# First norm of a decoder layer in two halves of the tokens, with the first weights loaded ahead of the context

## The reference

```python
x = x + attn(layernorm(x), ...)        # 16 heads of 128: q, k through a causal depthwise convolution of 4 taps,
                                       # silu and a norm; a decaying state S = (1-b) S + b v k^T; gate; Wo
x = x + xattn(layernorm(x), ctx, ...)  # query and key from ctx (128 wide), softmax over 256, applied to x
x = x + ffn(layernorm(x), ...)         # 2 shared and 16 routed experts, 4 of 16 chosen per token
```

## Time and profile before

| what | us |
|---|---|
| median of three runs | 595.95 |
| the profiled execution's own time | 597.41 |
| its span | 595.5 |
| TensorE busy | 557.4 (94%) |
| VectorE busy | 437.1 (73%) |
| ScalarE busy | 398.3 (67%) |
| GpSimd busy | 298.9 (50%) |

### The profile page before, as it was taken

The page is one execution under the profiler, slowest core; times in us unless marked ns, Lnnn a source line. Parts: engine busy times, 40 slices in busy tenths (PEclk is TensorE's granted clock), DMA queues, the critical chain, the costliest instruction groups (busy, mean ns, idle before and its releaser), DMA issues.

```text
span 595.5 us, 10331 instructions
## 1 busy us (share of the span) xinstructions
PE 557.4 (94%) x3392; PEld 488.2 (82%) x3392; DVE 437.1 (73%) x1046; ACT 398.3 (67%) x783; POOL 298.9 (50%) x201
## 2 busy tenths in 40 slices
PE   3899999999999999999999999897777799999996
PEld 1687889989989989989989988786566688888885
DVE  8778989989989988998998998968593433333334
ACT  4978988878978979879779778665531433343331
POOL 2434756746746646656666563301041655556542
PEclk9998999999999999999999999999998899999999
DMA  6122032032032032032031020110002433333311
GB/s 206 29 107 81 0 117 81 1 116 81 2 117 81 2 116 81 2 116 75 8 116 56 27 97 23 59 29 1 0 1 70 149 105 107 104 123 113 108 62 70
DMA packets 16267, 42.23 MB, mean 71 GB/s; under 512 B 4544, under 2 KB 4800, under 8 KB 16224
## 3 DMA queue, kind: packets, MB, share of 16 engines
q1 hardware_dynamic: 16224, 41.69, 20.9%
HBM read 40.47 MB, written 1.21 MB: 70 GB/s over the span
## 4 chain that ended last, share of the span: by engine, by line
PE 83%; DVE 8%; ACT 4%; DMA 2%; issue 2%; SPq 1%; ACTq 0%; DVEq 0%
PE bank L1258 20%; PE bank L1260 19%; PE bank L1259 19%; PE bank L1254 15%; PE bank L1396 5%; PE bank L1384 4%; ACT tok L624 2%; DMA xbias<-in_xb 1%; DMA w_raw<-in_w 1%; DVE stats L976 1%; DVE xT_lo L911 1%; DVE gated_lo L1158 1%; ACT values L538 0%; DVE x L1248 0%; DVE raw L995 0%
## 5 line engine op out<-in xcount | busy, mean ns | idle before, releaser
L1258 PE MATMUL bank<-xT_lo,w_hi 128*128 128x512 f32 x336 | 140.0, 417 | 3.6 <-DVE conv L1149 1.3
L1260 PE MATMUL bank<-xT_hi,w_hi 128*128 128x512 f32 x336 | 132.3, 394 | 0.0
L1259 PE MATMUL bank<-xT_hi,w_lo 128*128 128x512 f32 x336 | 131.8, 392 | 0.0
L425 POOL TENSOR_TENSOR gated_lo<-gated,gated_hi 128x512 fp32r<-128x512 f32 x30 | 38.7, 1290 | 116.5 <-ACT gated_hi L644 112.8
L624 ACT ACTIVATE tok<-bank,nmr,rstd 128x128 f32<-128x128 f32 x256 | 91.0, 504 | 2.1 <-DVE nmr L891 2.1
L502 POOL TENSOR_TENSOR gate<-conv,tap 128x512 f32<-128x512 f32 x36 | 46.4, 1291 | 84.5 <-DVE conv L1149 71.4
L1258 PEld LDWEIGHTS bank<-xT_lo,w_hi 128*128 128x128 f32 x336 | 63.5, 189 | 18.8 <-DVE conv L995 3.2
L1260 PEld LDWEIGHTS bank<-xT_hi,w_hi 128*128 128x128 f32 x336 | 63.3, 188 | 14.2
L420 POOL TENSOR_TENSOR conv<-tap,conv 128x506 f32<-128x506 f32 x32 | 61.9, 1934 | 21.8 <-DVE conv L995 21.8
L420 POOL TENSOR_TENSOR raw<-tap,raw 128x506 f32<-128x506 f32 x32 | 61.9, 1934 | 20.3 <-DVE raw L995 16.3
L1259 PEld LDWEIGHTS bank<-xT_hi,w_lo 128*128 128x128 f32 x336 | 63.7, 190 | 9.6
(11 more groups left out here) (167 smaller groups left out, 1358.3 us busy)
## 6 DMA issues: line engine op xcount, KB each, us to landing
w_raw<-in_w SPq DMA_DIRECT2D x34, 384.0 KB, 4.4
obet<-obet_rows SPq DMA_DIRECT2D x16, 768.0 KB, 4.2
tap<-route_rows SPq DMA_DIRECT2D x16, 512.0 KB, 3.6
wv_raw<-in_wv SPq DMA_DIRECT2D x8, 256.0 KB, 4.8
wo_raw<-in_wo SPq DMA_DIRECT2D x8, 256.0 KB, 4.9
x<-in_x SPq DMA_DIRECT2D x2, 512.0 KB, 4.6
out_x<-x SPq DMA_DIRECT2D x4, 256.0 KB, 2.4
raw<-in_ctx SPq DMA_DIRECT2D x1, 512.0 KB, 5.4
```

The costliest lines, as they stand in the source:

```text
L425: nc.gpsimd.tensor_tensor(gated_lo[:, cc], gated[:, c * N:(c + 1) * N], gated_hi[:, cc].bitcast(F32), ALU.subtract).then_inc(gated_lo_read ...
L1258: nc.tensor.matmul(o, l_hi, r_lo, start=start, stop=False, skip_group_check=loose)
L1259: nc.tensor.matmul(o, l_lo, r_hi, start=False, stop=False, skip_group_check=loose)
L1260: return nc.tensor.matmul(o, l_hi, r_hi, start=False, stop=stop, skip_group_check=loose)
```

## The change

Nothing is computed in another way; instructions and loads change places.

- SyncE: the identity, head 0's weights and the first value weights are issued right behind x; the context's three loads follow, then the parameters, beta's weights and bias.
- VectorE: statistics and factors are made for half 0 alone (four tiles), then its norm and its low part, then the same for half 1. The mask's copies move from behind the norm to behind head 0's second taps, the low part of half 1 and of beta's weights between its first and second taps.
- ScalarE: the norm of half 0 and its copies come right behind the weights' high part; the norm of half 1, then the first taps of head 0, then half 1's copies.
- TensorE: the transposes of half 0, two context products, the query product of half 0, values unit 0, the transposes of half 1, values unit 1, the other two context products, and the query product of half 1.
- The context products use banks 4 and 5 twice, since banks 6 and 7 now hold values; products 2 and 3 wait until ScalarE has emptied the bank.
- GpSimd waits for the factors of half 0 only before its first low parts, and for both before the low part of head 1's weights.

```diff
--- before.py
+++ after.py
@@ -270,12 +270,7 @@
         def _(sp):
             for c in range(NCH):
                 sp.dma_start(x[:, c * T:(c + 1) * T], x_in[:, c * T:(c + 1) * T]).then_inc(ld_x[c], 16)
-            sp.dma_start(xw, xw_in).then_inc(ld["ctx"], 16)
-            sp.dma_start(ctxT, ctx_in).then_inc(ld["ctx"], 16)
-            sp.dma_start(xb[:, :], xb_in).then_inc(ld["ctx"], 16)
             sp.dma_start(ident[:, :], ident_in).then_inc(ld["const"], 16)
-            sp.dma_start(wb, wb_in).then_inc(ld["beta"], 16)
-            sp.dma_start(bb, bb_in).then_inc(ld["beta"], 16)
 
             def load_weights(g, k):
                 s = k % 2
@@ -315,8 +310,13 @@
                              ).then_inc(ld["wo"], 16)
 
             load_weights(0, 0)
+            load_values(0, 0)
+            sp.dma_start(xw, xw_in).then_inc(ld["ctx"], 16)
+            sp.dma_start(ctxT, ctx_in).then_inc(ld["ctx"], 16)
+            sp.dma_start(xb[:, :], xb_in).then_inc(ld["ctx"], 16)
             load_params(0, 0)
-            load_values(0, 0)
+            sp.dma_start(wb, wb_in).then_inc(ld["beta"], 16)
+            sp.dma_start(bb, bb_in).then_inc(ld["beta"], 16)
             load_weights(0, 1)
             load_params(0, 1)
             load_weights(0, 2)
@@ -432,9 +432,10 @@
                                         ALU.subtract).then_inc(wo_lo_ready, 1)
 
 
-            pool.wait_ge(ln_rstd, NCH)
+            pool.wait_ge(ln_rstd, 1)
             split_low(0, 0)
             low_values(0, 0)
+            pool.wait_ge(ln_rstd, NCH)
             split_low(0, 1)
             last_tap(0, 0, range(2 * NCH))
 
@@ -550,11 +551,9 @@
             def context_out(u):
 
                 act.wait_ge(x_qk_full, u + 1)
-                nc.scalar.activation(attT[:, u * N:(u + 1) * N], bank[4 + u][:, :], ACT.Identity,
+                nc.scalar.activation(attT[:, u * N:(u + 1) * N], bank[4 + u % 2][:, :], ACT.Identity,
                                      bias=xb[:, u // NCH:u // NCH + 1]).then_inc(x_qk_ready, 1)
 
-            act.wait_ge(ld["beta"], 32)
-            nc.scalar.activation(wb_hi, wb, ACT.Copy).then_inc(small_split, 1)
             def high(g, k):
 
                 s = k % 2
@@ -651,18 +650,21 @@
                 nc.scalar.activation(wo_hi[:, w], wo_raw[:, :], ACT.Copy).then_inc(wo_hi_ready, 1)
 
             high(0, 0)
+            half_norm(0, 0)
+            half_out(0, 0, xT_hi)
             act.wait_ge(ld_wv[0], 16)
             nc.scalar.activation(wv_hi[:, 0:N], wv_raw[:, 0:N], ACT.Copy).then_inc(wv_hi_ready, 1)
             context_out(0)
             context_out(1)
-            for c in range(NCH):
-                half_norm(0, c)
+            act.wait_ge(ld["beta"], 32)
+            nc.scalar.activation(wb_hi, wb, ACT.Copy).then_inc(small_split, 1)
+            half_norm(0, 1)
+            first_taps(0, 0, (0,))
+            half_out(0, 1, xT_hi)
             context_out(2)
-            for c in range(NCH):
-                half_out(0, c, xT_hi)
             context_out(3)
             high(0, 1)
-            first_taps(0, 0, (0, 1))
+            first_taps(0, 0, (1,))
 
             for c in range(NCH):
                 act.wait_ge(b_full, c + 1)
@@ -912,27 +914,19 @@
                                             ALU.subtract).then_inc(ln_split, 1)
 
             obet_zero = steps.did(nc.vector.memset(obetT, 0.0))
-            a = steps.did(nc.vector.memset(dmask[:, :], 0.0))
-
-            for t in range(TT):
-                dve.wait_ge(ld_x[t // G], 16)
-                ins = x_stats(t)
-            steps.after(steps.did(ins))
-            norm_factors(TT, D).then_inc(ln_rstd, NCH)
-            for c in range(NCH):
+            dmask_zero = steps.did(nc.vector.memset(dmask[:, :], 0.0))
+
+            def first_half(c):
+                for t in range(G * c, G * (c + 1)):
+                    dve.wait_ge(ld_x[c], 16)
+                    ins = x_stats(t)
+                steps.after(steps.did(ins))
+                norm_factors(G, D, G * c).then_inc(ln_rstd, 1)
                 half_norm(0, c)
 
-            dve.wait_ge(ld["const"], 16)
-            steps.after(a)
-            dm = dmask[:, :].rearrange("p (b c) -> p b c", b=B)
-            for b in range(B):
-                nc.vector.tensor_copy(dm[:, b, 0:P], ident[:, :])
-                ins = nc.vector.tensor_copy(dm[:, b, L:L + P], ident[:, :])
-            ins.then_inc(dmask_ready, 1)
-            for c in range(NCH):
-                half_low(0, c)
-            dve.wait_ge(small_split, 1)
-            nc.vector.tensor_tensor(wb_lo, wb, wb_hi.bitcast(F32), ALU.subtract).then_inc(b_lo_ready, 1)
+            first_half(0)
+            half_low(0, 0)
+            first_half(1)
 
             def context_max(e):
                 dve.wait_ge(x_energy, e + 1)
@@ -1028,7 +1022,18 @@
                 nc.vector.tensor_tensor(xs, c_ring[u % 2][:, :], xs, ALU.add).then_inc(c_drained, 1)
 
             taps(0, 0, 0)
+            half_low(0, 1)
+            dve.wait_ge(small_split, 1)
+            nc.vector.tensor_tensor(wb_lo, wb, wb_hi.bitcast(F32), ALU.subtract).then_inc(b_lo_ready, 1)
             taps(0, 0, 1)
+
+            dve.wait_ge(ld["const"], 16)
+            steps.after(dmask_zero)
+            dm = dmask[:, :].rearrange("p (b c) -> p b c", b=B)
+            for b in range(B):
+                nc.vector.tensor_copy(dm[:, b, 0:P], ident[:, :])
+                ins = nc.vector.tensor_copy(dm[:, b, L:L + P], ident[:, :])
+            ins.then_inc(dmask_ready, 1)
 
             dve.wait_ge(b_ready, NCH)
             steps.after(obet_zero)
@@ -1274,16 +1279,10 @@
             def context_qk(u):
                 pe.wait_ge(ld["ctx"], 48)
                 s, c = divmod(u, NCH)
-                mm(bank[4 + u][:, :], xw[:, s * P:(s + 1) * P], ctxT[:, c * N:(c + 1) * N],
+                if u > 1:
+                    pe.wait_ge(x_qk_ready, u - 1)
+                mm(bank[4 + u % 2][:, :], xw[:, s * P:(s + 1) * P], ctxT[:, c * N:(c + 1) * N],
                    True, True).then_inc(x_qk_full, 1)
-
-            context_qk(0)
-            context_qk(1)
-            pe.wait_ge(ld["const"], 16)
-            context_qk(2)
-            for c in range(NCH):
-                half_transpose(0, c)
-            context_qk(3)
 
             def energies(b):
                 if b < 2:
@@ -1465,8 +1464,17 @@
                         if j:
                             ins.then_inc(p_full, 1)
 
+            pe.wait_ge(ld["const"], 16)
+            half_transpose(0, 0)
+            context_qk(0)
+            context_qk(1)
             pe.wait_ge(ln_split, KT)
             project_in(0, 0, 0, (0,))
+            values_of(0, 0, (0,), 1)
+            half_transpose(0, 1)
+            values_of(0, 0, (1,), 1, 1)
+            context_qk(2)
+            context_qk(3)
             pe.wait_ge(ln_split, KT * NCH)
             project_in(0, 0, 0, (1,))
             beta_logits()
@@ -1476,7 +1484,6 @@
             project_in(0, 1, 0)
 
             pe.wait_ge(x_qk_ready, 2 * NCH)
-            values_of(0, 0, (0, 1), 1)
             pe.wait_ge(b_tok_ready, 1)
             to_tokens(0, 0, range(2 * NCH))
```

## The result

The first series of executions put the changed kernel at 605.02 us (median of 4; 604.70 to 606.32) against 595.96 us before (4; 595.76 to 599.21): a ratio of 1.0143 with a 95% interval of 1.0105 to 1.0181. It is slower, as forecast, but by 9.1 us instead of 5.4, and the time lies above the range (603.3 us). Over all executions timed in this study, that of later sections included, the medians are 604.75 us (10 executions) and 596.96 us (54), 7.8 us apart.

A forecast was written before the change was run, and what follows sets the result against it. The prediction took TensorE's chain as the bound, the end of head 1's query product setting when the dense part begins. Lead-in order +4.6 and mask copies +0.8 us gave +5.4 on the 595.95 us median: 601.3 us, range 598.2 to 603.3.

The forecast's parts named there:

- What bounds the start: Lead-in: end of head 1's query product sets when the dense part begins; moving values out of TensorE's slack gains 0.
- q(half 1): TensorE's query product of the second token half in the lead-in, forecast to start at 23.5 instead of 18.86 us.
- Start of the transposes: Half 0's first transposes on TensorE: forecast at 10.9 us, 3.1 us earlier than before; 9.8 us without the GpSimd lock.
- the first norm operation would get through: VectorE's norm of half 0: first operation starts unheld at 8.65 us, GpSimd holds the second to 10.9 us.
- The rival: VectorE's norm: late weights make GpSimd miss the second operation; transposes at 9.8 us, +4.3, 600.2 us; chance 18%.
- From there to q(half 1): Lead-in after the first transposes: low part of half 0 at 14.1, second transposes 19.2, query product 23.5 us; +4.6 us.
- TensorE's slow pace: Cold TensorE at the start: first four microseconds of work near half speed, leaving 0.65 us at half 0's transposes.
- The mask's copies: VectorE behind head 0's second taps: two copies get through, GpSimd holds six; gate product +0.8 us, between 0 and 1.1.
- The half-speed stretch: TensorE at 1.2 GHz in 48 to 49 us; rival: it goes or a second comes, mostly 599.6 or 602.9 us; 14%.
- tells some 0.2%, 1.2 us, from no change: Whole kernel: the claimed resolution of a measurement, some 0.2% or 1.2 us; forecast set against the runs' median 595.95 us.
- The rest shifted alike: Everything behind the gate product, itself some 5.4 us later, was to shift by the same amount.
- Faster and unchanged: Whole kernel: faster if values are the real bound, 594.4 us, 5%; unchanged if the loss is made up, 597.1 us, 4%.

The follow-up runs named there:

- values_back: Changed kernel with both values units back behind head 1's query product, all else as changed; 606.29 us (one execution).
- pool_late: Changed kernel with GpSimd's first low part waiting for VectorE's norm of half 0 instead of its factors; median 604.62 us (4).
- low_first: Changed kernel with half 1's copies ahead of head 0's first taps on ScalarE, its low part ahead of VectorE's taps; 606.49 us (one execution).
- low_values: Changed kernel with half 1's copies and low part ahead of the taps, and the values back behind head 1's query product; 603.38 us (one execution).
- mask_back: Changed kernel with the mask's eight copies right behind VectorE's norm of half 0, where it waits for ScalarE; median 603.43 us (4).
- after: The changed kernel itself, all parts of the change against the kernel before; 605.02 us in the first series, ratio 1.0143.
- mask_late: Kernel before with one part of the change alone, the mask's copies behind head 0's second taps; 599.37 us (one execution).
- best: Kernel before, norm unhalved, ScalarE's norm ahead of context outputs, GpSimd's low part after VectorE's norm, context products and mask copies moved; 595.17 us (12), ratio 0.9966.

## Why the prediction was right and wrong

- *What bounds the start*: right. The query product of head 1, the taps, the scaling and the statistics set when the dense part begins; moving the values from behind it won nothing, and putting them back (values_back) lost nothing at q(half 1).
- *Start of the transposes*: right, 11.04 against 10.9 us, and its cause shown by pool_late (1.24 us for the lock; forecast 1.1). That the first norm operation would get through failed in the first profile: it was the one held, for 2.00 us, and the second followed. The time still fitted by luck, since GpSimd began at 8.62 us instead of 8.80 and took 1.80 us instead of 1.93. The rival didn't occur: the split was done at 8.47 us.
- *From there to q(half 1)*: right, 23.30 against 23.5 us, on two paths of equal length, as low_first, values_back and low_values show. Measured at the key product, the term was 4.57 us for a forecast 4.6. One step on the way was too short: TensorE's slow pace was taken as four microseconds and lasted until 16.6 us, 5.6 us from its start. It cost next to nothing, since ScalarE's norm of half 1 ended only at 19.15 us and TensorE came to the transposes at 19.21; in low_first, where the pace rose 0.7 us earlier, TensorE waited 0.39 us there.
- *The mask's copies*: right in kind, 0.5 us for 0.8. As forecast, two copies got through and GpSimd held the next until about 29.55 us; but five were left then and not six, and VectorE's taps began at 31.11 us instead of 31.35. Without the copies they would have begun at 30.67 us by mask_back (30.54 us, with transposes 0.13 us earlier) and not at 30.6.
- *The half-speed stretch*: here the prediction failed. It was kept out of the sum, as if it would stay as it was, with a rival that was to move it by at most one stretch either way. In the first profile the changed kernel has one at 34 us where the other has one at 47, which is even, and one more at 426 us, worth 1.65 us, a place that the prediction didn't look at.
- *The reference, and "tells some 0.2%, 1.2 us, from no change"*: wrong. From profile to profile the loss is 7.4 us (5.04 at the gate product, 0.75 over the heads, 1.65 for the stretch). The sum was put on top of a median of 595.95 us, while the profiled execution took 597.41; the four executions of the kernel before that the series had are at the low end of what it does (median 595.96, but 596.96 over 54), and those 54 spread over 7.1 us, with mean clocks between 0.984 and 0.994. The forecast of +5.4 us compares with about 4.5 to 5.9 us at equal clock, with 7.8 us over everything, and with 9.1 us in the series.
- *"The rest shifted alike"*: wrong by the growth between head 1 and head 15, 0.75 us. Every profile of the changed kernel and its variants takes 312.68 to 312.75 us for this way, every one of the kernel before and its variants 311.93 to 312.03, wherever the half-speed stretches fall. About half of it is one place, a wait for VectorE's taps, which the kernel before hasn't (its profile has no wait of TensorE there):

```profile
88.42 0.50 PE L1263 MATMUL bank<-xT_lo,w_hi 128*128 128x512 f32 x1 [0.21 <-DVE raw L989]
```

  Against the kernel before, TensorE loses 0.35 us there and another 0.2 at the same product two heads later, at 134.4 us. Why VectorE's taps come later there, and the small rest, stay open. So does what makes a standstill end in a half-speed stretch: behind that of 2.54 us in front of the last norm's first product, at 425.71 us in the changed kernel and at 419.97 us before, the clock fell in one and not in the other.
- *Faster and unchanged*: neither occurred. The limit named for the former, transposes at 7.8 us, was missed by over 3 us.

## What to carry to other kernels

Before work is moved forward into a lead-in, ask whether it was paid for where it stood: the values and three of four context products were free in the kernel before, and halving the norm made VectorE's chain of small dependent operations (2.4 us) run twice, one behind the other. Order the first norm by the engine that is late (here ScalarE stood behind context outputs nobody needed) and start GpSimd only when VectorE's operations between two SBUF tiles are through. And where TensorE's clock halves after a standstill, count a stretch as a term of the sum with its own spread, and compare kernels at equal mean clock, or up to a point that repeats, before a difference of one or two microseconds is believed.

## What the runs showed of the hardware

- The lock between GpSimd and VectorE takes copies too: a 128x128 float32 copy from SBUF to SBUF took 1.30 us beside GpSimd's last tap (L420) in after and mask_late, 1.31 in low_first, and 1.21 and 1.33 us beside its last tap and low part in best; otherwise 0.21 to 0.22 us. The prediction had this from the Trainium skill (SBUF — State Buffer, who interferes with whom) and no row; the rows agree.
- At the start TensorE runs at half pace, while the granted clock reads 1.00: in the changed kernel eight transposes took 1.94 us at 11.04 us and 1.10 us at 19.21 us. How long differs: by the spacing of the matmuls until 12.8 us in the kernel before (4.3 us from its first matmul), 16.6 us in the changed one (5.6 us) and 14.1 us in best (5.7 us).
- Half-speed stretches of about 3.4 us came at the same places, within 0.5 us, in two profiles each of two kernels, but one lasted twice as long; and variants that hardly differ there had one more or one less. One in front of the experts cost 1.6 us (49.97 to 50.01 us against 48.35 to 48.44). The kernel before spreads over 7 us (593.85 to 600.97), while its two profiles repeat within 0.2 us up to head 15.
